# Where the decays of the state-space scans are kept: SBUF in place of four PSUM banks

## The reference

```python
def step(h, inp):
    d_t, b_t, c_t, x_t = inp
    dA = jnp.exp(d_t[..., None] * A)
    h = dA * h + d_t[..., None] * b_t[:, None, :] * x_t[..., None]
    y_t = jnp.sum(h * c_t[:, None, :], axis=-1)
    return (h, y_t)
...
_, ys = jax.lax.scan(step, h0, xs)
y = jnp.swapaxes(ys, 0, 1) + Dp * x
y = _layernorm(y, ln_g, ln_b)
return jnp.einsum('bsd,ed->bse', y, W_out)
```

## Time and profile before

| what | us |
|---|---|
| median of 3 runs | 720.3 |
| lowest and highest | 720.24, 722.64 |
| the profiled execution | 720.35 |
| its span, first to last instruction | 718.5 |
| DVE busy in the span | 447.3 (62%) |
| PE busy | 535.5 (75%) |
| POOL busy | 373.4 (52%) |
| ACT busy | 308.4 (43%) |

### The profile page before, as it was taken

One profiled execution on the slowest core, in us unless ns is written; L12 is line 12 of the kernel. 1 busy time (PEld: TensorE's weight loads), 2 busy tenths in 40 slices (PEclk: granted clock), 3 DMA queues, 4 the chain that ended last, 5 costly groups with the idle time before them and its releaser, 6 DMA issues.

```text
span 718.5 us, 10709 instructions
## 1 busy us (share of the span) xinstructions
PE 535.5 (75%) x3309; PEld 378.0 (53%) x3309; DVE 447.3 (62%) x975; ACT 308.4 (43%) x628; POOL 373.4 (52%) x318
## 2 busy tenths in 40 slices
PE   3497878889788688777365779787895959999900
PEld 1032424335243335666354668676684748899900
DVE  1589999999999973379657475746361431222245
ACT  2455474856648342122132445454442413333327
POOL 1497978989788754113543354534444342333351
PEclk9999999999999988555556698999797978999955
DMA  5433435344462514463252544442434336689774
GB/s 160 148 120 139 155 133 192 125 165 155 161 189 106 205 61 89 89 99 67 57 139 44 162 150 146 149 170 92 141 126 152 110 132 201 218 284 296 252 227 132
DMA packets 87545, 106.63 MB, mean 148 GB/s; under 512 B 40912, under 2 KB 68816, under 8 KB 87360
## 3 DMA queue, kind: packets, MB, share of 16 engines
q1 hardware_dynamic: 78800, 93.08, 42.1%
q0 software_dynamic: 4320, 8.92, 3.6%
q10 hardware_dynamic: 4368, 3.93, 1.7%
HBM read 93.57 MB, written 12.34 MB: 147 GB/s over the span
## 4 chain that ended last, share of the span: by engine, by line
issue 30%; POOL 19%; PE 18%; DVE 14%; DMA 9%; ACT 4%; SPq 2%; another core or an unknown queue 1%; DVEq 0%; POOLq 0%; ACTq 0%
POOL hc L660 9%; PE pB L1058 6%; DMA wslot<-in_expert_w 5%; DVE h L1477 3%; PE pq L1071 3%; POOL xg_dram L760 3%; PE py L840 3%; POOL y_dram L769 2%; DVE u L1468 2%; ACT x_all L1430 1%; PE py L1058 1%; POOL bcs L613 1%; DMA y_dram<-dx,xin 1%; POOL bc_rest L605 1%; DMA Crep<-c_dram 1%
## 5 line engine op out<-in xcount | busy, mean ns | idle before, releaser
L660 POOL TENSOR_TENSOR hc<-h,Crep 128x1024 f32<-128x1024 f32 x64 | 150.0, 2355 | 23.7 <-DVE h L1477 22.6
L769 POOL DMA_INDIRECT y_dram<-dx,xin x71 | 68.8, 968 | 155.9 <-ACT dx L1354 146.7
L1058 PE MATMUL pB<-Crep,wslot 128*128 128x256 f32 (+1 forms) x556 | 121.7, 365 | 18.7 <-DMA wslot<-in_expert_w 10.3
L840 PE MATMUL py<-hc,ident 128*128 128x512 f32 x256 | 122.8, 608 | 4.3 <-POOL hc L660 4.3
L1058 PEld LDWEIGHTS pB<-Crep,wslot 128*128 128x128 f32 x556 | 92.7, 208 | 36.5 <-DMA wslot<-in_expert_w 13.1
L1468 DVE TENSOR_TENSOR u<-dx,pC 128x1024 f32<-128x1024 f32 x64 | 76.9, 1202 | 18.5 <-PE pC L829 18.5
L840 PEld LDWEIGHTS py<-hc,ident 128*128 128x128 f32 x256 | 49.4, 196 | 55.3 <-issue 42.1
L1791 DVE TENSOR_TENSOR Crep<-u,pB 128x512 f32<-128x512 f32 x35 | 24.0, 686 | 86.9 <-PE pB L1058 48.5
L829 PE MATMUL pC<-bcs,sel 96*128 96x512 bf16 x128 | 41.0, 403 | 45.0 <-DVE u L1468 39.8
L1477 DVE TENSOR_TENSOR_SCAN h<-pa,u 128x1024 f32<-128x1024 f32 x32 | 73.0, 2281 | 0.0
L1477 DVE TENSOR_TENSOR_SCAN h<-pB,u 128x1024 f32<-128x1024 f32 x32 | 73.0, 2281 | 0.0
(11 more groups left out here) (224 smaller groups left out, 948.2 us busy)
## 6 DMA issues: line engine op xcount, KB each, us to landing
wslot<-in_expert_w SPq DMA_DIRECT2D x46, 768.0 KB
Crep<-c_dram SPq DMA_DIRECT2D x64, 512.0 KB, 3.7
h<-m_dram SPq DMA_DIRECT2D x16, 256.0 KB
xin<-xg_dram SPq DMA_DIRECT2D x25, 130.0 KB
xbuf<-in_x_tok SPq DMA_DIRECT2D x8, 256.0 KB, 4.6
cT_st<-in_ctx_T SPq DMA_DIRECT2D x8, 256.0 KB, 4.6
dx<-in_ctx_T SPq DMA_DIRECT2D x8, 256.0 KB, 4.7
delta<-in_ctx_tok SPq DMA_DIRECT2D x32, 64.0 KB
```

Source lines behind the costliest of these rows:

```text
L660: nc.gpsimd.tensor_tensor(hc[:, K % 4], h[:, K % 3], Crep[:, K % 4].rearrange("p a t -> p (a t)"), ALU.mult).then_inc(hc_done, 1)
L769: nc.gpsimd.indirect_dma_start(out=y2_dram, out_offset=bass.IndirectOffsetOnAxis(ap=xin[:, i % NX, a, D:D + 1].bitcast(i32), axis=0), in_= ...
L840: last = nc.tensor.matmul(py[:], ident[:], hc[:, K % 4, i * CH:(i + 1) * CH], start=False, stop=(K % STEPS == STEPS - 1 and i == 1))
L1058: last = nc.tensor.matmul(bank[:, o * a * P:(o + 1) * a * P], wslot[:, i % NW, stage * F + f * P:stage * F + (f + 1) * P], xgT[i % 2][:, 0 ...
```

## The change

The tile `decay` is the first 2048 floats of each partition of `wslot`, seen as two buffers of 1024. `decay_exp` writes its two Exp there and `scan` reads there. The choice between `pa` and `pB` by the parity of K becomes a choice between the two buffers by the same parity. All waits stay as they are, and every engine has the same instructions in the same order. `pa` and `pB` are not touched by the steps any more, and nothing else is put in them there.

```diff
+        decay = wslot[:].rearrange("p n f -> p (n f)")[:, 0:4 * CH].rearrange("p (a t) -> p a t", a=2)
...
             def decay_exp(K):
                 c, k = K // STEPS, K % STEPS
-                bank = pB if K % 2 else pa
...
-                    last = nc.scalar.activation(bank[:, i], delta[:, c % 2], ACT.Exp, scale=Aneg[:, n:n + 1])
+                    last = nc.scalar.activation(decay[:, K % 2, i * CH:(i + 1) * CH], delta[:, c % 2], ACT.Exp, scale=Aneg[:, n:n + 1])
...
             def scan(K):
-                bank = pB if K % 2 else pa
...
-                nc.vector.tensor_tensor_scan(h[:, K % 3], bank[:].rearrange("p a t -> p (a t)"), u[:, K % 3], 0.0, ALU.mult,
+                nc.vector.tensor_tensor_scan(h[:, K % 3], decay[:, K % 2], u[:, K % 3], 0.0, ALU.mult,
                                              ALU.add).then_inc(h_done, 1)
```

## The result

The changed kernel takes 810.65 us in the median of 4 runs (808.91 to 816.94), the kernel before 721.47 in the same number (720.24 to 725.33). The ratio of the two is 1.1255, with a 95% interval of 1.1206 to 1.1304. Ratios and intervals here are of the fast runs alone (none over 1.5% above the fastest of its kernel), so they can differ a little from what the medians give. The profiled execution of the changed kernel took 809.77 us with a span of 808.0; that of the kernel before 720.35 and 718.5. So the span grew by 89.5 us, where the forecast said 86.4.

The account below looks back on a forecast made before the run. DVE was taken to bound the state-space stage (246.3 us), POOL following; scans and POOL's readers in one line, 291.8 + 37.9 + 3 = 332.7 us, add 86.4 to 720.35, giving 806.8 us, range 790 to 850.

Parts of the forecast that it names:

- The bound and the place: State-space stage: DVE sets it at 3.31 us a step, 246.3 us in all; nothing behind the stage changes.
- ACT: The 128 Exp: 700 ns each into SBUF against 682 into PSUM, all under cover, counted 0.
- The scan by itself: DVE's scan reading decays from SBUF instead of PSUM: counted 0, ends 20 ns either way, 1.3 us in 64.
- Case C: Rival: scans gain from a smaller fixed part reading SBUF; 716 us, chance 0.03.
- The scan beside POOL: Deciding term: a scan with both inputs in SBUF and POOL's SBUF readers exclude each other; step 4.56 us, not 3.31.
- Case A: Rival: the scan does not exclude POOL and nothing happens; 719 to 722, 720 us, chance 0.12.
- One sign that was named for it: Sign of the forecast being right: the scans' mean at 3.3 to 3.6 us in place of 2.28.
- The sum: Stage as one line: 291.8 for steps, 37.9 for POOL's other readers, 3 us for waits: 332.7, +86.4 us.
- The gates' chain: Last chunk of the stage, where DVE waits for PE: 3 us left for what of this stays.
- hc longer only where it stands behind a reader: Sign in POOL's hc: longer than 2.355 us only behind one of the five other POOL readers in a chunk.
- who gets the next turn: Scan or POOL first: does not matter for the sum, since h has three buffers and neither side can run off.
- Case B: Rival: in the stage TensorE falls to its lower clock and becomes the bound; 845 us, chance 0.10.

Follow-up runs that it names:

- e1: Changed kernel, decays still in SBUF, but u written to the freed PSUM banks, each product also waiting for the scan just ahead: 727.95 us.
- e2: Kernel before with one edit: each product waits for the scan just ahead of it; 731.07 us, ratio 1.0107.
- e3: Decays of odd steps in SBUF, those of even steps in PSUM as in the kernel before: 770.41 us, ratio 1.0656.
- e5: Changed kernel with hc halved: POOL weighs only the first of the two states of a step; 754.59 us.
- e7: Changed kernel with hc replaced by a POOL fill of SBUF that nobody reads, PE adding up x instead: 733.82 us.
- e4: Changed kernel where PE adds up only the first of the two states of each step: 809.75 us.

## Why the prediction was right

*The bound and the place.* Right. DVE set the stage at 3.31 us a step, and all of the loss lies between the first scan and the last hc; the rest of the kernel moved as a block, 2.5 us shorter in this pair of profiles, which no step of the prediction speaks of and which is within what single runs of one kernel differ.

*ACT.* Right: 712 ns for 700 taken, +30 over PSUM, 128 x 0.03 = 3.8 us of ACT, under cover but for the one wait of 0.7 us. e1 shows the price when nothing else is wrong: none that its stage of 250.6 us, against 250.9 in e2, would show.

*The scan by itself.* Right: the shortest scan with both inputs in SBUF takes 2276 ns; before, the mean is 2281 and the shortest 2265. Case C, a gain of 20 to 60 ns in each scan, is out. The fixed parts that the Trainium skill gives in "VectorE: DVE Perf Modes", section on the TRN2 errata (58 cycles from SBUF, 120 from PSUM), find no support in this form.

*The scan beside POOL.* Right, and this was the term. Case A, that a scan asks for its inputs at half the rate and leaves room, fell at once: the scan of 31.01 is 3.56 us long, where 3.5 was put as the point that decides. The exclusion is as whole for it as for the element-wise forms. e1, e3, e5 and e7 each take away one other cause. One sign that was named for it didn't come: the scans' mean is 2.85 us and not 3.3 to 3.6, because POOL's side took more than half of the waiting. By their own lengths 36 of the 64 scans were held, for 36 us in all, and 44 of POOL's hc and other readers, for 81.

*The sum.* The stage was put at 332.7 us and took 338.65, so it was 6 us too small, and the time 3.9 us too low (806.8 for 810.65). Two terms were off, in opposite directions. Taken by their own lengths (2.28 us for a scan, 2.355 for an hc), the scans and POOL's readers are at work for 323.5 us of the stage, and 3.4 more go between one and the next in gaps of some 0.1 us. That makes 326.9 for the line that the forecast put at 329.7. I gave the scan its full 2.28 and 0.07 for the hand-over, but where POOL is already waiting, the scan's last 0.2 us don't hold it up. And I took the line as never empty but for 3 us. It stood empty nine times for 11.8 us. The gates' chain has 3.95 of these, near the 3 I had left for it. The other eight, 0.4 to 1.4 us each, lie where DVE has a product or row work to do before its next scan while POOL has nothing to read, so DVE's row work was not wholly under cover. DVE's own idle time is larger (27.0 us over 18 times before a scan, for hc, since only three `h` buffers let it run ahead), but POOL works then and the line is not empty.

```profile
L1476 DVE TENSOR_TENSOR_SCAN h<-wslot,u x64: 2276/2682/4397, 27.7 to 358.6; 128x1024 f32<-128x1024 f32 x64
```

The scans' range of 2276 to 4397 ns shows that the rhythm is not the even one of the sum: some scans wait for nothing and some for nearly a whole hc. "hc longer only where it stands behind a reader" was wrong accordingly: hc waited more than the scan did, 0.76 against 0.57 us in the mean. I had said that who gets the next turn doesn't matter for the sum. That held within 2%.

*Case B, TensorE's clock.* The granted clock of the stage fell from 0.98 to 0.84, so part of the work ran at 1.2 GHz, as that case said it might. DVE's idle time before products, which is for PE, grew from 18.5 to 35.9 us. But PE never became the bound: e4 left out half of its adding up, ran at a granted clock of 0.71 in the stage, and got 3.9 us back. So B was true of the clock and false of the time.

*What stays open.* Why this stage's chunks differ (from one chunk's first scan to the next one's 37 us at the start and 41 to 44.5 later, where before these were 29 to 30) was not followed up either.

## What to carry to other kernels

Before an operand moves from PSUM to SBUF, look at what the other engines do beside its reader: a VectorE operation with both inputs in SBUF and a GpSimd operation that reads SBUF take turns, and their lengths add up where they overlapped. One input in PSUM, whichever of the two, is enough to keep them apart, and so is a GpSimd operation that only writes. A single short operation in the trace that takes ten times its length beside a GpSimd one, as `lfg` did, shows this for a loop that has none of it yet. The price is then the two lengths laid behind one another in every step, less what either engine had to spare.

## What the runs showed of the hardware

- By its own length, a held scan starts 0.13 to 0.14 us before the record of the operation that held it ends (36 scans), and a held POOL operation 0.19 to 0.22 us before the scan's record ends (44 operations).
- The exclusion is the same at two rates: the scan takes 2.2 ns per column and blocks as the 1.2 ns per column forms do.
- Waits go into the records as busy time: POOL's busy time in the stage rose from 199 to 293 us with no work added, and DVE's from 228 to 268.
- Small operations are hit as well. POOL's 128x128 selection among its constants (0.29 us in the kernel before) took 1.61 beside a scan. First the kernel before, then the changed one:

```profile
56.38 0.29 POOL L672 TENSOR_SCALAR_AFFINE_SELECT tri<-tri 128x128 f32<-128x128 f32 x1
```

```profile
66.79 1.61 POOL L673 TENSOR_SCALAR_AFFINE_SELECT tri<-tri 128x128 f32<-128x128 f32 x1
```
